# Last cross attention of a decoder: q and k projected apart, scores over 64 rows, two units issued together

## The reference, cut to what matters

```python
xn = layer_norm(x, g1, b1)                 # x: the context
ln_lat = layer_norm(latents, g2, b2)       # latents: the state
q = ln_lat @ Wq
kv = jnp.concatenate([xn, ln_lat], axis=1) @ Wkv
k, v = jnp.split(kv, 2, axis=-1)
...
weight = jnp.einsum('bhld,bhnd->bhln', q * scale, k * scale)   # scale = 64 ** -0.25
weight = jnp.where(full_mask[:, None, None, :], weight, neg)
weight = jax.nn.softmax(weight, axis=-1)
out = jnp.einsum('bhln,bhnd->bhld', weight, v)
return out @ Wout
```

## Time and profile before

| | |
|---|---|
| median of 3 runs | 1938.68 us (1937.98 to 1938.98) |
| span of the profiled execution | 1932.0 us |
| TensorE busy | 1736.0 us, 90% of the span |
| VectorE busy | 1378.8 us, 71% |
| ScalarE busy | 1340.0 us, 69% |
| GpSimd busy | 837.3 us, 43% |
| mean granted clock of TensorE | 0.960 |

### The profile page before, as it was taken

How to read it: one execution, slowest core, us unless ns; L and a number is a source line. 1 busy time by engine, 2 the same in 40 slices (tenths; PEclk the granted TensorE clock), 3 DMA queues, 4 the chain that set the end, 5 groups by cost and what they waited for, 6 DMA issues and landing times. The chain is left out here.

```text
span 1932.0 us, 40599 instructions
## 1 busy us (share of the span) xinstructions
PE 1736.0 (90%) x13884; PEld 1294.5 (67%) x13945; DVE 1378.8 (71%) x3901; ACT 1340.0 (69%) x5411; POOL 837.3 (43%) x998
## 2 busy tenths in 40 slices
PE   6999999999888898789999999615889999999998
PEld 6886558889655565246688888404556777777777
DVE  4667886777888898988844444595998656566665
ACT  3447986565899996159977777442988666666666
POOL 2235770000566785147733333121776433333345
PEclk9999999999988999789999999866999999999999
DMA  7000000000000000000000000200000000000000
GB/s 285 1 1 1 2 2 2 1 2 2 2 1 2 2 2 2 1 1 2 2 2 1 2 1 2 117 0 1 1 2 2 1 1 1 1 1 1 1 1 23
DMA packets 5819, 22.98 MB, mean 12 GB/s; under 512 B 624, under 2 KB 2672, under 8 KB 4720
## 3 DMA queue, kind: packets, MB, share of 16 engines
q1 hardware_dynamic: 5616, 20.39, 2.7%
HBM read 19.34 MB, written 1.05 MB: 11 GB/s over the span
## 5 line engine op out<-in xcount | busy, mean ns | idle before, releaser
L1394 POOL TENSOR_TENSOR a_probs<-a_probs,a_rinv 128x512 f32<-128x512 f32 x352 | 365.7, 1040 | 318.0 <-DVE a_rinv L1238 314.5
L1047 ACT ACTIVATE a_probs<-bank,a_negmax 128x128 f32<-128x128 f32 x896 | 324.8, 434 | 12.9 <-DVE a_negmax L1218 12.8
L1394 POOL TENSOR_TENSOR c_probs<-c_probs,c_rinv 128x512 f32<-128x512 f32 x192 | 200.1, 1042 | 163.5 <-DVE c_rinv L1238 160.4
L889 PEld LDWEIGHTS bank<-const,a_probs 128*128 128x128 f32 x1408 | 159.0, 144 | 134.0 <-issue 110.2
L1047 ACT ACTIVATION_READ_ACCUMULATOR a_probs<-bank,a_negmax 128x1 f32 x896 | 237.5, 275 | 0.0
L889 PE MATMUL bank<-const,a_probs 128*128 128x128 f32 x1408 | 231.4, 288 | 1.9 <-DVE a_probs_t L1245 0.9
L1422 POOL TENSOR_TENSOR a_rstd<-a_ve,neg_half 128x1 f32<-128x1 f32 x128 | 70.2, 549 | 341.1 <-DVE a_ve L1296 340.9
L1218 DVE TENSOR_REDUCE a_negmax<-bank 128x4 f32<-128x512 f32 x224 | 152.0, 680 | 20.5 <-PE bank L857 16.6
L857 PE MATMUL bank<-a_kz,a_qk 32*128 32x512 f32 x512 | 148.1, 655 | 2.2 <-DVE a_probs L1216 1.6
L1238 DVE RECIPROCAL a_rinv<-a_rsum 128x4 f32<-128x4 f32 x352 | 59.7, 170 | 113.7 <-ACT a_probs L1043 107.8
L1245 DVE COPY a_probs_t<-bank 128x512 f32<-128x512 f32 x176 | 120.5, 684 | 25.8 <-PE bank L889 24.7
(11 more groups left out here) (254 smaller groups left out, 4418.9 us busy)
## 6 DMA issues: line engine op xcount, KB each, us to landing
w_L_ffn<-in_L_ffn SPq DMA_DIRECT2D x1, 3184.0 KB, 20.4
w_L_xattn<-in_L_xattn SPq DMA_DIRECT2D x1, 2112.0 KB, 29.5
w_L_xattn<-in_L_xattn SPq DMA_DIRECT2D x1, 2050.0 KB, 9.9
w_L_attn<-in_L_attn SPq DMA_DIRECT2D x1, 1345.5 KB, 23.1
w_L_attn<-in_L_attn SPq DMA_DIRECT2D x1, 1157.0 KB, 6.7
ctx_t<-in_ctxT SPq DMA_DIRECT2D x1, 1024.0 KB, 13.0
w_L_attn<-in_L_attn SPq DMA_DIRECT2D x2, 512.0 KB, 14.7
ctx<-in_ctx SPq DMA_DIRECT2D x1, 1024.0 KB, 13.3
```

The lines of the kernel that those rows point to most:

```text
L889: mm = pe.transpose(bank[:, j * S:(j + 1) * S], Pb[:, n % PB, j * S:(j + 1) * S], ident)
L1047: op = act.activation(p, bank_of("scores", n)[:, j * width:(j + 1) * width], ACT.Exp, bias=negmax[:, n % PB, j:j + 1], accum_out=rsum[:, n ...
L1394: pool.tensor_tensor(p, p, along(rinv[:, n % PB, 0:heads], 512 // heads), ALU.mult).then_inc(sems["norm_done"], 1)
```

## The change

- q and k are projected apart. `wide_q` and `wide_k` (the transposes of the packed weights, two heads to a chunk of 128) take the place of `score_w`; 16 transposes with the identity make them between the parts, and ACT copies each bank once it is full. A step now has q0, q1 (four matmuls of 128 columns each) and k0 to k3 (two of 256 columns each), where k goes to a new tile KX.
- The scores of a head multiply 64 rows of Q64 with 64 rows of KX. Heads 2c and 2c+1 lie in the upper and lower rows; their matmuls are issued one after the other and go to the banks of two units. Both units of a pair are issued in the slot of the even one. The scores have four banks instead of three.
- Values of two units are issued together, behind the odd one (`closes`), and copied by ACT in one instruction of 256 columns instead of two of 128.
- The table `EARLY` has new places: q0 in the slot of c (10 ahead), k0 9, k1 8, q1 7, k2 6, k3 5, v0 4, v2 3, v1 2, v3 1; before, it was c 10, q0 and q1 9, q2 and q3 8, v1 6, v0 5, v2 and v3 4. ACT copies c, q0, k1, k2, v0, v1; DVE k0, q1, k3, v2, v3.

```diff
@@ -37,7 +37,7 @@
     "h64c": [("q0", 9, "act"), ("q1", 7, "act"), ("k0", 6, "dve"), ("k1", 5, "dve"), ("v0", 4, "act"), ("v1", 2, "act")],
-    "h64m": [("c", 10, "act"), ("q0", 9, "act"), ("q1", 9, "dve"), ("q2", 8, "act"), ("q3", 8, "dve"), ("v0", 5, "act"), ("v1", 6, "dve"), ("v2", 4, "act"), ("v3", 4, "dve")],
+    "h64m": [("c", 10, "act"), ("q0", 10, "act"), ("k0", 9, "dve"), ("k1", 8, "act"), ("q1", 7, "dve"), ("k2", 6, "act"), ("k3", 5, "dve"), ("v0", 4, "act"), ("v2", 3, "dve"), ("v1", 2, "act"), ("v3", 1, "dve")],
     "ffn": [],
@@ -87,7 +87,7 @@
     "h64c": {"scores": (0, 1, 2, 3), "second": (4,), "use": (6, 7), "values": (5,)},
-    "h64m": {"scores": (0, 1, 2), "second": (4,), "use": (6, 7), "values": (5,)},
+    "h64m": {"scores": (0, 1, 2, 3), "second": (4,), "use": (6, 7), "values": (5,)},
     "ffn": {"scores": (0, 1, 2), "second": (3, 4), "use": (5, 6, 7)},
...
@@ -198,7 +198,7 @@
             now = max(m - LEAD[stage].get(kind, LEAD[stage]["all"]), at, before + 1)
-            if stage == "scores" and kind in H8:
+            if stage == "scores" and kind in H8 + ("h64m",):
                 now = at if i % 2 else max(now, at + 1)
@@ -206,6 +206,11 @@
 
+    def closes(self, m):
+
+        s, i = self.units[m]
+        return i == 3 if self.kind(s) in H8 else i % 2 == 1 if self.kind(s) == "h64m" else True
+
     def later(self, what, s):
...
@@ -599,7 +604,8 @@
                 V64 = sb(tag + "v64", [P, 2, nkeys // S, 1024], scope=scope)
-                Q64 = sb(tag + "q64", [P, 2, 16, S], scope=scope)
+                Q64 = sb(tag + "q64", [P, 2, 8, S], scope=scope)
+                KX = sb(tag + "kx", [P, 2, 8, 2, S], scope=scope)
                 KV = sb(tag + "kv", [P, G, 2, S], scope=scope)
@@ -817,17 +823,32 @@
                                 for j in range(4):
-                                    mm = pe.matmul(bank[:, j * S:(j + 1) * S], score_w[:, 4 * i + j, :], KV[:, b, 1, :], start=True, stop=True)
+                                    mm = pe.matmul(bank[:, j * S:(j + 1) * S], wide_q[:, 4 * i + j, :], KV[:, b, 1, :], start=True, stop=True)
+                            elif name[0] == "k":
+                                for j in range(2):
+                                    mm = pe.matmul(bank[:, j * 256:(j + 1) * 256], wide_k[:, 2 * i + j, :], KV[:, b, :, :].rearrange("p a k -> p (a k)"), start=True, stop=True)
                             else:
...
                         s, i, kind, b = plan.unit(n)
-                        if kind in H8 and i % 2:
+                        if kind in H8 + ("h64m",) and i % 2:
                             return
...
                         bank_free("scores", n)
+                        if kind == "h64m":
+                            after_reader(pe, s, f"q{i // 4}")
+                            after_reader(pe, s, f"k{i // 2}")
+                            bank_free("scores", n + 1)
+                            for j in range(2):
+                                for odd in range(2):
+                                    rows = slice(64 * odd, 64 * odd + 64)
+                                    mm = pe.matmul(bank_of("scores", n + odd)[:, j * 256:(j + 1) * 256], Q64[rows, plan.ring(s, 2), i + j, :],
+                                                   KX[rows, plan.ring(s, 2), i + j, :, :].rearrange("p a k -> p (a k)"), start=True, stop=True)
+                                    if j == 1:
+                                        mm.then_inc(sems["scores_ready"], 1)
+                            return
                         if i == 0:
@@ -865,10 +886,6 @@
                                 mm = pe.matmul(bank[:, j * S:(j + 1) * S], Qz[:, plan.ring(s, 2), 2 * i + j // 2, j % 2, :], K64[:, plan.ring(s, 2), 2 * i + j // 2, :], start=True, stop=True)
-                        elif kind == "h64m":
-                            for j in range(2):
-                                mm = pe.matmul(bank[:, j * 256:(j + 1) * 256], Q64[:, plan.ring(s, 2), 2 * i + j, :],
-                                               KV[:, b, :, :].rearrange("p a k -> p (a k)"), start=True, stop=True)
                         elif kind == "moe":
@@ -906,16 +923,19 @@
                         s, i, kind, b = plan.unit(n)
+                        if not plan.closes(n):
+                            return
                         stage = plan.copier(n)
-                        if i == 0:
+                        if kind == "h64m":
+                            after_reader(pe, s, f"v{i // 4}")
+                            after_reader(pe, s, f"v{2 + i // 4}")
+                        elif i == 0 or kind in H8:
 
...
 
-                            if i < 3:
-                                return
                             for m in range(n - 3, n):
@@ -936,11 +956,12 @@
                         else:
-                            for c in range(2):
-                                for j in range(2):
-                                    h = 2 * i + j
-                                    mm = pe.matmul(value_bank[64 * j:64 * j + 64, 0:S], V64[:, plan.ring(s, 2), c, h * 64:(h + 1) * 64],
-                                                   pt[:, (2 * j + c) * S:(2 * j + c + 1) * S], start=c == 0, stop=c == 1)
+                            for j in range(2):
+                                for c in range(2):
+                                    for odd in range(2):
+                                        h = 2 * (i - 1 + j) + odd
+                                        mm = pe.matmul(value_bank[64 * odd:64 * odd + 64, j * S:(j + 1) * S], V64[:, plan.ring(s, 2), c, h * 64:(h + 1) * 64],
+                                                       PT[:, (n - 1 + odd) % PT_RING, (2 * j + c) * S:(2 * j + c + 1) * S], start=c == 0, stop=c == 1)
                         mm.then_inc(sems["values_ready"], 1)
@@ -999,6 +1020,9 @@
                             op = act.activation(gatewT[:, b % 2, :], bank[0:NE, 0:P], ACT.Copy)
+                        elif kind == "h64m" and name[0] == "k":
+                            i = int(name[1])
+                            op = act.activation(KX[:, plan.ring(s, 2), 2 * i:2 * i + 2, :, :].rearrange("p c a k -> p (c a k)"), bank[:, :], ACT.Copy)
                         elif kind == "h64m" and name[0] == "q":
...
@@ -1091,7 +1115,7 @@
                         else:
-                            op = act.activation(OT[:, plan.ring(s, 2), i, :], value_bank[:, 0:S], ACT.Copy)
+                            op = act.activation(OT[:, plan.ring(s, 2), i - 1:i + 1, :], heads_view(value_bank[:, 0:2 * S], 2), ACT.Copy)
                         op.then_inc(sems["out_taken"], 1)
@@ -1155,6 +1179,9 @@
                             op = dve.tensor_tensor(R[:, b % R_RING, :], bank[:, 0:D], X[:, b, :], ALU.add)
+                        elif kind == "h64m" and name[0] == "k":
+                            i = int(name[1])
+                            op = dve.tensor_copy(KX[:, plan.ring(s, 2), 2 * i:2 * i + 2, :, :].rearrange("p c a k -> p (c a k)"), bank[:, :])
                         elif name[0] == "k":
@@ -1514,26 +1541,26 @@
                               banks, q_in, fc1_q, fc2_q, load_context)
-            score_w = sb("score_w", [P, 16, D], scope=scope)
-            score_w_full, score_w_taken = sem("score_w_full"), sem("score_w_taken")
+            wide_q = sb("wide_q", [P, 8, P], scope=scope)
+            wide_k = sb("wide_k", [P, 8, P], scope=scope)
+            wide_full, wide_taken = sem("wide_full"), sem("wide_taken")
             with nc.Block() as block:
...
                     pe.wait_ge(w_in["L3_xattn"], 16)
-                    q, k = (part(w["L3_xattn"], "L3_xattn", n) for n in ("WqT", "WkT"))
-                    for h in range(16):
-                        rows, c = slice(64 * (h % 2), 64 * (h % 2) + 64), h // 2
-                        pe.matmul(banks[2 * (h // 8) + h % 2][:, (h // 2 % 4) * D:(h // 2 % 4 + 1) * D],
-                                  q[rows, c * D:(c + 1) * D], k[rows, c * D:(c + 1) * D], start=True, stop=True).then_inc(score_w_full, 1)
+                    for u in range(4):
+                        of = part(w["L3_xattn"], "L3_xattn", ("WqT", "WkT")[u // 2])
+                        for j in range(4):
+                            c = 4 * (u % 2) + j
+                            mm = pe.transpose(banks[u][:, j * P:(j + 1) * P], of[:, c * P:(c + 1) * P], ident)
+                        mm.then_inc(wide_full, 1)
 
...
                 def _(act):
-                    act.wait_ge(score_w_full, 16)
-                    for half in range(2):
-                        for odd in range(2):
-                            bank = banks[2 * half + odd]
-                            heads = score_w[:, 8 * half:8 * half + 8, :].rearrange("p (c o) d -> p c o d", o=2)[:, :, odd, :]
-                            act.activation(heads, heads_view(bank[:, :], 4), ACT.Copy, scale=0.125).then_inc(score_w_taken, 1)
+                    for u in range(4):
```

(13 more changed lines are left out.)

## The result

The changed kernel takes **1947.72 us** (median of 4 runs, 1946.14 to 1950.94) against 1938.33 for the kernel before on the same chip: a ratio of 1.0053, 95% interval 1.0039 to 1.0067. The forecast was 4.5 us faster; it came out 9.4 us slower. The profiled execution spans 1944.3 us against 1932.0.

The account below looks back on a forecast made before the run. TensorE was taken to bound the kernel; periods -2.1, both ends -1.0 and preparation -1.4 sum to -4.5 us, so 1932.0 becomes 1927.5, plus 6.7 around it: 1934.2 us. Forecast's own range 1928 to 1941; overall range 1918 to 1951.

Parts of the forecast that it names:

- What bounds the kernel: Last cross attention: TensorE busy 240.00 of 240.00 us at full clock, so its instruction stream is the time.
- Score groups 1.06: Scores of two units in 64-row pairs take 1.06 us a group; 4.24 a step for 7.68 before.
- Values 1.01: Values of two units issued together take 1.01 us a group; 4.04 a step for 4.72 before.
- The wait in slot 6, 1.78: Slot 6 from a step's first unit: q0 waits 1.78 us on TensorE for ScalarE's copy of c.
- v3's start: v3 waits 0.38 us for q0's bank, starting 5.06 us after the start of slot 6's transposes (T).
- Period 25.21: Step of the last cross attention: 22.67 us of TensorE work plus 2.54 of waits, 0.14 less than before.
- Both ends -1.0: First and last steps of the last cross attention: given -1.0 us together.
- Preparation -1.4: Weight preparation between the parts: transposes with copies as banks fill end 1.4 us earlier; bounds 0 and -2.
- The clock falling behind the wait: Rival: slot 6's wait lowers TensorE's clock; +12 to +18 us at 10 to 15 waits, 1946 to 1952; chance 0.20.
- Pairs overlapping worse: Rival: 64-row score groups take 1.30 us, total 1950, or 1976 without overlap; chance 0.10.
- The gain that shows if ScalarE came to c earlier: Rival's case: waits of 1.78 and 0.38 go, -35 us, about 1900; whole gain rival 0.22, 0.05 below 1918.
- The change doesn't do what it says: Rival: something else orders TensorE as before, 1938 us; chance 0.03.

Follow-up runs that it names:

- experiment 9: Changed kernel with c 11 slots ahead, v1 copied by VectorE and v2 by ScalarE, and in the first step k3, v1, v2, v3 all by ScalarE: 1919.39 us.
- Experiment 5: Changed kernel with score matmuls over all 128 rows instead of 64, leaving out the separation of a chunk's two heads: 1986.19 us, ratio 1.0245.
- experiment 2: Changed kernel with only c due one slot earlier, 11 ahead instead of 10: 1925.51 us, ratio 0.9941.
- experiment 7: experiment 2's kernel, with the copies of k3, v2 and v3 on ScalarE in the last cross attention's first step alone: 1923.15 us, ratio 0.9919.
- experiment 8: experiment 2's kernel, with VectorE copying v1 and ScalarE v2 instead of the other way round: 1922.04 us, ratio 0.9907.
- Experiment 6: Kernel before with the new preparation alone (16 transposes, each bank copied when full; products of Wq and Wk left out): 1938.73 us, ratio 1.0008.
- experiment 3: Kernel before with q0 alone moved into c's slot, 10 ahead instead of 9: 1972.89 us, ratio 1.0184.

## Why the prediction was wrong, step by step

- **What bounds the kernel: right.** TensorE's stream was the time, and experiment 9 is at 239.71 of 240 us again. The forecast missed by 13.8 us of the span without the stretch up to the preparation (-4.5 against +9.3): 6.5 in the periods, 5.0 in the two ends, 2.3 around the preparation.
- **Score groups 1.06: right inside, wrong at the border.** They took 1.07, and the order in them did not matter. But L857's 1.06 in the earlier trace rows is start to start, and so holds nothing of what the projection ahead loses: 0.95 to 0.96 instead of 0.86 (k0, 1585.01 to 1585.96), and from q1 by y to the scores 2.95 (1589.89 to 1592.84), where the prediction's terms make 2.83 (0.90 + 0.14 + 1.79). This is the mis-sized term: 4 x 0.10 = 0.40 a step, 6 us over 15. Alone it makes the period 0.26 longer than before where 0.14 less was forecast. Experiment 5 shows that it belongs to the change of shape.
- **Values 1.01: right**, 1.02. The k projections at 0.86, taken from the chain's L870, came out at 0.86 to 0.87 where no score group follows. The transposes of the odd slots took 0.48 instead of 0.44 plus the wait of 0.08 counted for three of them: together 0.04 better each.
- **The wait in slot 6, 1.78: right** (c at 1580.34, q0 at 1582.23: 1.89, of which c itself takes 0.11), as was v3's start. q0 took 0.96 and not 0.90, but since v3 still began at T+5.06 this only shortened v3's wait. v3 itself then took 0.96 and not 0.86; in experiment 2, where it has no wait ahead, it takes 0.86.
- **Period 25.21: wrong, 25.71.** 0.40 for the entries, 0.10 for v3 and 0.08 for the eight groups of scores and values at 0.01 each, less 0.12 for the transposes, is 0.46 of the 0.50 missed. So a step is 0.36 longer than before, not 0.14 shorter: 13 such periods from the 1st to the 14th y are +4.7, and the two short ones at the end -0.2, which is the +4.4 of the table.
- **Both ends -1.0: wrong, +4.0.** The prediction had no row behind this term: it looked at the end, and put the first step aside as lying in the attention before it. The first step lies beside the masks of the attention, and its waits were 5.8 us where there had been none. Experiment 2 takes 2.57 off (the c order), experiment 7 another 1.03 (k3, v2, v3 on VectorE); 0.38 is left. Together with experiment 8's table the 1.03 shrinks to 0.15.
- **Preparation -1.4: right in place (-1.6), wrong in worth.** Experiment 6 has no gain at all left in the median (+0.08%, interval -0.03 to +0.20%): the loop's start usually gives it back, at the lower clock. The prediction took the preparation's end as the end of its effect.
- **The rivals.** The clock falling behind the wait: not in the changed kernel, where it was 1.00 behind all 14 waits of 1.6; behind slightly longer waits in experiment 3 twice in 14. So it happens, and for this loss it was too rare here. (The kernel before had more rows on this than the earlier trace rows show: of six waits of 1.6 to 1.7 in loop A, from 534.14 to 641.57, five were followed by a granted clock of 0.65 to 0.70. Behind waits of that length in the changed kernel's steps there was none; why, no run shows.) That the measured 1947.72 lies within this rival's 1946 to 1952 is chance. Pairs overlapping worse: refuted. The gain that shows if ScalarE came to c earlier, "about 1900": its mechanism was right and its size not, since not all of the 2.16 a step was had: against the changed kernel experiment 2 got 1.48 a step and 22 us in all, experiment 9 1.70 a step and 28 us. "The change doesn't do what it says" fell at once.

The loss of 9.3 is thus 2.5 - 1.6 around the preparation, 4.0 in the first steps and 4.4 in the periods. Of these, the cost of the score groups' borders and 3.6 of the first steps' 4.0 are shown by runs; the smaller parts of the period are read from the traces, and the loop's start is shown as a tendency only.

## What to carry to other kernels

When a stage is moved, read the order in which the copying engine comes to it: here one table entry (c and q in one slot, both behind ScalarE's last copy) held back the gain, and taking one dependency away only showed the next one behind it. Cost the borders of a tiled group as well as its inside, by comparing the same neighbour ahead of a tiled and of an untiled group. And give the first step of a pipelined loop a sum of its own: it runs beside another stage's load, where the engine with room in the steady state may have none (in the changed kernel VectorE was busy for 5.76 of the 6.00 us ahead of 1502, and for 154.32 of 240.00 in the steps).

## What the runs showed of the hardware

- Two 64-row float32 matmuls of 256 columns on different row halves run side by side: four take 1.07 us with the change of shape behind them, over all rows 1.82. The order in which they are queued does not matter (1.07 with both orders).
- A change of tile shape between neighbouring groups costs 0.10 us of TensorE, from full to 64 rows (0.96 against 0.86) and, as read from neighbouring groups without a run of its own, from full to half the columns (1.82 against 1.72; before, 0.96 for L870 against 0.86 for L822).
- Of 14 equal waits of 1.99 us (experiment 3) two were followed by a lower granted clock, 0.63 and 0.57 in a stretch of 4 us, the second at a cost of 1.56 us; the others by none. All 14 waits of 1.6 us in the changed kernel's steps left it at 1.00, one of 1.62 in experiment 8 was followed by 0.57, at a cost of 1.63 us, and the same wait in experiment 9 by 1.00.
